# First pass, first four tiles: K and V computed chunk by chunk of Wk and Wv, eight tiles of x in buffers of their own

## The reference

```
src = layernorm(x)
q, k, v = src @ Wq + bq, src @ Wk + bk, src @ Wv + bv     # 16 heads of 64
Q, K = elu(q) + 1, elu(k) + 1
KV = einsum('bshd,bshm->bhdm', K, v)                       # sum over all rows
Z  = 1 / (einsum('bshd,bhd->bsh', Q, K.sum(axis=1)) + eps)
o  = einsum('bshd,bhdm,bsh->bshm', Q, KV, Z) @ Wo + bo
x1 = layernorm(src + o) * g1 + be1
u  = layernorm(x1 + gelu(x1 @ W1 + b1) @ W2 + b2) * g2 + be2
xa = x + u
out = xa + layernorm(xa) @ Wf.T + pooled(layernorm(xa)) @ disha
```

## Time and profile before

| | us |
|---|---|
| time, median of 3 runs (lowest, highest) | 1622.37 (1622.12, 1623.51) |
| the profiled execution's own time | 1624.31 |
| its span on the slowest core (core 5), first to last instruction | 1622.8 |
| spans of the eight cores | 1617.1 to 1622.8 |
| PE busy in the span | 1539.5 (95%) |

### The profile page before, as it was taken

How to read it: one execution, slowest core, us unless ns; L and a number is a source line. 1 busy time by engine, 2 the same in 40 slices (tenths; PEclk the granted TensorE clock), 3 DMA queues, 4 the chain that set the end, 5 groups by cost and what they waited for, 6 DMA issues and landing times.

```text
span 1622.8 us, 28100 instructions; the slowest of 8 cores (1617.1 to 1622.8 us)
## 1 busy us (share of the span) xinstructions
PE 1539.5 (95%) x9892; PEld 928.7 (57%) x9892; DVE 928.4 (57%) x1042; ACT 598.4 (37%) x1010; POOL 502.7 (31%) x438
## 2 busy tenths in 40 slices
PE   2699999999789999999999999999999999999995
PEld 1254544554356666666666666666666666666662
DVE  1466665665626574756657474755657475665314
ACT  1244555544533233333323333342323333332321
POOL 3464544545344222222222222222122222222101
PEclk9799999999899999999999999999999999999998
DMA  9776655457772201111110201111120111111011
...
DMA packets 52183, 135.60 MB, mean 84 GB/s; under 512 B 5968, under 2 KB 14160, under 8 KB 52048
## 3 DMA queue, kind: packets, MB, share of 16 engines
...
## 4 chain that ended last, share of the span: by engine, by line
PE 92%; issue 2%; DVE 2%; DMA 2%; POOL 1%; ACT 1%; SPq 0%; DVEq 0%; ACTq 0%; POOLq 0%
PE psH L1100 27%; PE psY L1081 27%; PE psY L444 13%; PE psS L673 7%; PE psS L493 6%; PE psS L415 6%; PE psS L659 1%; PE psS L547 1%; PE psH L423 1%; DMA qt_s<-arena 1%; PE psS L436 1%; PE psS L568 1%; DMA arena<-x 1%; PE psY L415 1%; PE psY L493 0%
## 5 line engine op out<-in xcount | busy, mean ns | idle before, releaser
L1100 PE MATMUL psH<-arena 128*128 128x256 bf16 x4096 | 531.6, 273 | 1.4 <-ACT arena L558 1.4
L1081 PE MATMUL psY<-arena 128*128 128x512 bf16 x2048 | 525.8, 379 | 0.4 <-DVE arena L601 0.4
L1006 ACT ACTIVATE arena<-psH,arena 128x256 bf16<-128x256 f32 x512 | 243.4, 475 | 733.3 <-PE psH L1100 731.4
L1100 PEld LDWEIGHTS psH<-arena 128*128 128x128 bf16 x4096 | 398.5, 98 | 131.0 <-issue 1.6
L1081 PEld LDWEIGHTS psY<-arena 128*128 128x128 bf16 x2048 | 200.3, 98 | 133.7 <-issue 1.6
L444 PE MATMUL psY<-arena 128*128 128x512 bf16 x1024 | 236.5, 386 | 16.3 <-DMA arena<-Wk 10.1
L589 DVE RECIPROCAL arena<-arena 128x512 f32<-128x512 f32 x56 | 187.4, 3346 | 29.8 <-ACT arena L579 29.8
L444 PEld LDWEIGHTS psY<-arena 128*128 128x128 bf16 x1024 | 100.2, 99 | 135.1 <-issue 25.6
L680 DVE TENSOR_TENSOR arena<-psS,arena 128x512 f32<-128x512 f32 x64 | 44.1, 689 | 168.1 <-PE psS L673 168.1
L502 DVE TENSOR_TENSOR arena<-psS,arena 128x512 f32<-128x512 f32 x60 | 41.3, 689 | 151.6 <-PE psS L493 151.4
L673 PE MATMUL psS<-arena 128*128 128x512 bf16 x512 | 122.2, 383 | 2.6 <-ACT arena L668 2.6
...
## 6 DMA issues: line engine op xcount, KB each, us to landing
arena<-x SPq DMA_DIRECT2D x64, 512.0 KB, 4.3
xb_s<-arena SPq DMA_DIRECT2D x32, 512.0 KB, 3.4
...
arena<-xb_s SPq DMA_DIRECT2D x32, 512.0 KB, 3.2
out<-arena SPq DMA_DIRECT2D x32, 512.0 KB, 2.9
arena<-qt_s SPq DMA_DIRECT2D x16, 512.0 KB, 3.2
...
```

What stands on the lines that cost most here:

```text
L1006: sc.activation(hT[n % 3][:, :], hbank[n % 2], AF.Gelu, bias=b1c[:, c:c + 1]).then_inc(b_g, 1)
L1081: ii = te.matmul(ybank[k], hT[n % 3][:, (k // 2) * P:(k // 2 + 1) * P], w2_v[c][:, (k % 2) * HALF:(k % 2 + 1) * HALF], start=(c == 0), sto ...
L1100: ii = te.matmul(hbank[n % 2], w1_v[c // NCH][:, w, (c % NCH) * P:(c % NCH + 1) * P], x1T[i % 2][:, w, :], start=(w == 0), stop=(w == NCH ...
```

## The change: what it does

Loads and buffers: tiles 2 to 7 of x get buffers of their own (`xe`, in the part of SBUF in which W2's chunks 16 to 27 land later), so that SP issues x0 to x3 at the start, x4 and x5 once Wk is in, x6 and x7 once Wv is in. The rows be2 and three small constants are issued after Wv has landed and no longer at the start. For tiles 0 to 7 be2 is added in place in the x buffer, after that tile's norm, and stored from there; `xbst` is used from tile 8 on. On POOL the four first k_sum come ahead of all x_be2. Tiles 1 and 3 get their own z and e buffers (`zf1`, `ebf1`), tiles 2 and 3 their own K buffers (`kx`).

Weights: each chunk of Wk and Wv has its own semaphore. PE takes chunk w for tiles 0 and 1 as it lands (`part`: two matmuls), with K of tile 2 following from chunk 5 on, then K of tile 3; V of tiles 0 and 1 by chunk of Wv; then V of tiles 2 and 3, and tile 4. For these tiles K and V lie in psK, psV and psH in turn. From tile 5 on the loop over tiles is the old one.

```diff
 def k_bank(t): return [psK, psV, psH.ap(), psK][t] if t < 4 else psK      # new
 def v_bank(t): return [psV, psH.ap(), psK, psV][t] if t < 4 else psV      # new
...
 def sync_a(sy):
-    for t in range(T):
-        if t >= 2:
-            sy.wait_ge(a_xb, t - 1)
-            sy.dma_start(xb_d[t - 2], xbst[:, :]).then_inc(s_xbst, 16)
-            sy.wait_ge(a_src, t - 1)
-        sy.dma_start(xbuf[t % 2][:, :], x_d[t * P:(t + 1) * P, :]).then_inc(s_x[t % 2], 16)
...
+    for t in range(1, 4):
+        x_load(t)
+    for dst, src in [(bqc, bqc_d), (bk1b, bkb_d)]:
+        sy.dma_start(dst[:, :], src).then_inc(s_const, 16)
+    sy.wait_ge(s_wk[NCH - 1], 16)
+    x_load(4)
+    x_load(5)
+    sy.wait_ge(s_wv[NCH - 1], 16)
+    for dst, src in [(be2b, be2_d), (onesb, one_d), (b1c, b1_d), (bvc, bvc_d)]:
+        sy.dma_start(dst[:, :], src).then_inc(s_rows, 16)
+    x_load(6)
+    x_load(7)
+    for t in range(8):
+        x_keep(t)
         if t == 1:
+            for u in range(2):
+                sy.wait_ge(s_x01[u], 16)
+                sy.wait_ge(a_src, u + 1)
+                x_load(8 + u)
+    for t in range(10, T):
+        x_keep(t - 2)
+        sy.wait_ge(a_src, t - 1)
+        x_load(t)
...
 def pool_a(gp):
     def x_be2(t):
...
+        if t >= 9:
+            gp.wait_ge(s_xbst, 16 * (t - 8))
+        if t < 8:
+            gp.wait_ge(a_src, t + 1)
+        gp.tensor_tensor(xbst[:, :] if t >= 8 else x_buf(t)[:, :], x_buf(t)[:, :],
+                         be2b[:, :], ALU.add).then_inc(a_xb, 1)
...
+    for t in range(4):
+        k_sum(t)
     x_be2(0)
     x_be2(1)
     for t in range(T):
         if t + 2 < T:
             x_be2(t + 2)
-        k_sum(t)
+        if t >= 4:
+            k_sum(t)
...
 def pe_a(te):
+    def part(t, w, ps, wgt, done):
+        for nh in range(2):
+            ii = te.matmul(ps[:, nh * 512:(nh + 1) * 512],
+                           srcT[0][:, w, t * P:(t + 1) * P],
+                           wgt[:, w, nh * 512:(nh + 1) * 512],
+                           start=(w == 0), stop=(w == NCH - 1))
+        if w == NCH - 1:
+            ii.then_inc(done, 1)
+
     src_tr(0)
-    for t in range(T):
+    src_tr(1)
+    for w in range(NCH):
+        if w == 0:
+            te.wait_ge(a_ev, 2)
+        te.wait_ge(s_wk[w], 16)
+        part(0, w, k_bank(0), wk_v, a_k)
+        part(1, w, k_bank(1), wk_v, a_k)
+        if w == 4:
+            src_tr(2)
+        if w == 5:
+            te.wait_ge(a_ev, 3)
+            for u in range(6):
+                part(2, u, k_bank(2), wk_v, a_k)
+        if w >= 6:
+            part(2, w, k_bank(2), wk_v, a_k)
+    src_tr(3)
+    te.wait_ge(a_ev, 4)
+    te.wait_ge(a_z, 1)
+    proj(3, k_bank(3), wk_v, a_k)
+    te.wait_ge(a_z, 3)
+    for w in range(NCH):
+        te.wait_ge(s_wv[w], 16)
+        part(0, w, v_bank(0), wv_v, a_v)
+        part(1, w, v_bank(1), wv_v, a_v)
+    src_tr(4)
+    te.wait_ge(a_z, 4)
+    proj(2, v_bank(2), wv_v, a_v)
+    te.wait_ge(a_vb, 2)
+    kv_sum(te, 0)
+    proj(3, v_bank(3), wv_v, a_v)
+    kv_sum(te, 1)
+    src_tr(5)
+    te.wait_ge(a_ev, 5)
+    te.wait_ge(a_vb, 3)
+    proj(4, psK, wk_v, a_k)
+    kv_sum(te, 2)
+    te.wait_ge(a_vb, 4)
+    proj(4, psV, wv_v, a_v)
+    kv_sum(te, 3)
+    te.wait_ge(s_wq, 16 * NCH)
+    q_proj(te, 0)
+    q_proj(te, 1)
+    for t in range(5, T):
```

More of the change, by code:

```diff
@@ L98, in build_nc @@
         ebf = VB(W + 51200, D)
+        xe = [VF(2048 * (16 + 2 * k), D) for k in range(6)]
+        kx = [VB(2048 * 28, D), VB(2048 * 29, D)]
+        zf1, ebf1 = VF(2048 * 14, D), VB(2048 * 30, D)
         slot = [VF(W + 4096 * k, D) for k in range(6)]
@@ L204, in qbuf, with k_bank, v_bank @@
             return qs1 if j == 1 else qs
+        def k_bank(t):
+            return [psK, psV, psH.ap(), psK][t] if t < 4 else psK
+        def v_bank(t):
+            return [psV, psH.ap(), psK, psV][t] if t < 4 else psV
         q_last = [sbank[0], ybank[2], sbank[0], ybank[3]]
@@ L210, in q_bank, with x_buf @@
             return sbank[0] if n < NCH * (NG - 2) else q_last[n % 4]
[L215 to L227 removed]
+        def x_buf(t):
+            return xe[t - 2] if 2 <= t < 8 else xbuf[t % 2]
@@ new lines, in k_buf, with z_buf, e_buf, x_done @@
+        def k_buf(t):
+            return kx[t - 2] if t in (2, 3) else kbf[t % 2]
+        def z_buf(t):
+            return zf1 if t in (1, 3) else zf
+        def e_buf(t):
+            return ebf1 if t in (1, 3) else ebf
+        def x_done(eng, t):
+            if 2 <= t < 8:
+                eng.wait_ge(s_xe[t - 2], 16)
+            else:
+                eng.wait_ge(s_x[t % 2], 16 if t < 2 else 16 * (t // 2 - 2))
+        def k_free(eng, t, done):
+            if t >= 6:
+                eng.wait_ge(done, t - 1)
+            elif t >= 4:
+                eng.wait_ge(done, t - 3)
@@ L316, in act_a @@
             evac(0)
-            for t in range(T):
-                if t + 1 < T:
+            evac(1)
+            rstd(2)
+            rstd(3)
+            evac(2)
+            evac(3)
+            for t in range(4):
+                k_exp(t)
+            rstd(4)
+            rstd(5)
+            v_out(0)
+            v_out(1)
+            evac(4)
+            v_out(2)
+            v_out(3)
+            evac(5)
+            sc.wait_ge(a_mem, 6)
+            for t in range(4, T):
+                if 5 <= t < T - 1:
                     evac(t + 1)
-                if t + 2 < T:
+                if 5 <= t < T - 2:
                     rstd(t + 2)
@@ L325, in act_a @@
                     q_store(sc, t // 4 - 2, 1)
+                k_exp(t)
+                if 5 <= t < T - 4:
+                    q_exp(sc, 2 * (t - 4))
                 if t == 4:
-                    sc.wait_ge(a_mem, 6)
-                k_exp(t)
-                if 4 <= t < T - 4:
-                    q_exp(sc, 2 * (t - 4))
+                    rstd(6)
                 v_out(t)
-                if 4 <= t < T - 4:
+                if t == 4:
+                    q_exp(sc, 0)
+                if t < T - 4:
                     q_exp(sc, 2 * (t - 4) + 1)
@@ L386, in dve_a @@
             norm(1)
+            stats(2)
+            stats(3)
+            norm(2)
             v.wait_ge(s_const, 32)
@@ L389, in dve_a @@
             v.tensor_scalar(bq1c[:, :], bqc[:, :], 1.0, None, ALU.add).then_inc(a_mem, 1)
-            stats(2)
-            for t in range(T):
-                if t + 2 < T:
+            norm(3)
+            k_in(0)
+            k_in(1)
+            k_out(0)
+            k_in(2)
+            k_out(1)
+            k_in(3)
+            k_out(2)
+            k_out(3)
+            stats(4)
+            stats(5)
+            norm(4)
+            norm(5)
+            for t in range(4, T):
+                if 5 <= t < T - 2:
                     norm(t + 2)
@@ L395, in dve_a @@
                 k_out(t)
-                if 4 <= t < T - 4:
+                if t == 4:
+                    stats(6)
+                    norm(6)
+                if t < T - 4:
                     q_out(v, 2 * (t - 4))
```

94 lines of the change are left out of this document (47 added, 47 removed).

## The result

The changed kernel takes 1608.98 us (median of 4 runs, 1608.0 to 1609.15), the kernel before 1622.24 us in 4 runs taken beside it (1622.12 to 1623.51). The ratio is 0.9915, 95% interval 0.9898 to 0.9932: faster by 13.3 us (0.8%), clear of the noise. The forecast was 1594.9 us with a range of 1588 to 1604, so the sign was right and the gain was half of the 27.4 us expected.

A forecast was written before the change was run, and what follows sets the result against it. PE's work bounds from tile 5 on; before, PE idles 46.4 us. Core 6's K of tile 5 moves from 94.75 to 66.5 us, ending at 1593.9; plus 1.4 spread, plus 1.5, minus 1.9 gives 1594.9 us, range 1588 to 1604.

The forecast's parts named there:

- K5: Start of K of tile 5 on PE, forecast at 66.5 us in place of 97.6 on core 5.
- the bound by which the small constants pay for x2: Loads at the start: moving the small constants away makes up for loading x2, so Wk lands at 26.2 us.
- rival 1: Wq gets half the DMA engines, lands at 68.5 us; K of tile 5 at 74.9, time 1603.3 us; chance 12%.
- rival 2: V of tiles 0 and 1 also at half clock, ending at 52.2 us, 7.2 late; time 1601 us; chance 6%.
- waits of PE on Wk and Wv in several short pieces: Expected sign in the profile after: PE waits briefly for weight chunks, ending near 28 and 44 us.
- Supply of x: Loop, x10 on: load, add, store, norm chain over 11.25 us a tile stalls PE; 1633 us at 13; chance 3%.
- 1 us of room at norm(6): DVE after K of tile 4: norm(6) done 1 us before src_tr(6) needs it at 66 us, costing nothing.
- The in-place add costs POOL what the old one did: POOL, tiles 0 to 7: adding be2 within the x buffer was taken to cost no extra time.
- a stall of 0 to 2 us: PE at src_tr(4), waiting for norm(4) on DVE, expected about 45 us; stall of 0 to 2 us.
- 1.4 us for the slowest core: Spread of the new tile 5 start between cores: half of the old 2.8 us, added to 1593.9 for 1595.3.
- The forecast's own case: Whole kernel: the forecast holds with a time of 1588 to 1599 us; chance 73%.
- rivals 1 to 3: Rival 1, rival 2, and a larger gain: K of tile 5 at 63.7, 1590.7 us; below 1588, chance 4%.

The follow-up runs named there:

- tiny adds: The changed kernel with POOL's in-place adds of be2 for tiles 0 to 7 covering one column of 1024, waits and stores kept; 1601.68 us, ratio 0.9866.
- be2 early: The changed kernel with be2 loaded behind x5 on its own semaphore, POOL's first adds waiting for it alone; 1602.09 us, ratio 0.9855.
- ACT order: The changed kernel with v_out(4) and q_exp(0) put ahead of rstd(6) in ACT's list; 1605.1 to 1605.9 us, ratio 0.9891.

## Why the prediction was right in sign and wrong in size

**Right.** The account of what bounds the kernel held: PE's work from tile 5 on is unchanged (297.1 to 297.5 us from K5 to the middle part on every core before, and on the four late cores after), and the gain is how much earlier the loop is done. Wk had landed by 25.87 us, when SP issues x4 (forecast 27.9, lower bound 26.2), and Wv by 41.78, when it issues be2 (forecast 43.7):

```profile
25.87 0.81 SPq L258 DMA_DIRECT2D arena<-x  x2
41.78 0.33 SPq L280 DMA_DIRECT2D arena<-be2r  x1
```

Both are 2 us early, as the bound by which the small constants pay for x2 would have it. Wq is seen where PE gets to it in time: its waits end at 59.1 to 62.0 us in the later experiments (forecast 62.6), so rival 1, Wq at 68.5, did not come. Rival 2, half clock until tile 3's V, did not come either: the granted clock over the first 81 us is 0.92, and K of tile 3 takes 3.61 us for 16 matmuls, the time at full clock. But its premise was not put to the test, nor did the "waits of PE on Wk and Wv in several short pieces" come: PE waited for Wk on no core and for Wv 0.7 us at most (core 2), since it started on chunks that had landed and was slow at first. Supply of x never held up PE in the loop. The W2 and Wo loads gave nothing back.

**Wrong, the step that decides.** "norm(6) comes behind K of tile 4 on DVE: ... k_in, k_exp, k_out, stats, rstd and norm take 7 to 9 us ... All of this costs nothing on that count, with 1 us of room at norm(6)", and with it "The in-place add costs POOL what the old one did". The add does cost POOL the same (2.36 us each), but not DVE. k_out was priced by its usual 1.2 us, and took 8.35 on core 4 beside adds in a row. In place of 1 us of room there was a 9.48 us wait, and it fell on q_proj(1), which the forecast took to run back to back with q_proj(0): it waits for a PSUM bank through q_exp(0), and ACT's list has rstd(6) ahead of that. So the step has two parts: k_out(4) held up for 7.1 us, and 2.4 us of waiting for the bank that come even without that, as tiny adds shows. Tiny adds (the wait down to 2.36 us) and be2 early (6.8 us back, nothing left out) show that it was the adds; ACT order shows how the wait reaches PE. The forecast had a hint in its own figures: it gives norm as 0.8 to 3.0 us and did not ask what made the long ones.

**Wrong, the smaller terms, on core 4.** The forecast had PE at the first q_proj at 61.5 us, and it was there at 65.55. Of these 4.0 us, 2.8 are src_tr(4), at 47.78 in place of 45.0 ("a stall of 0 to 2 us" was 3.41), and 1.3 the half clock that followed (48.59: 16 matmuls in 4.53 us). Wq's wait of 1.1 us fell away behind it. After the long wait q_proj and src_tr ran at half clock (granted 0.50 from 76 to 80 us): 3.37 and 0.85 us from start to start in place of 1.73 and 0.45, 2.0 us. So 66.5 + 4.0 - 1.1 + 9.5 + 2.0 = 80.9, with 81.14 measured. The forecast allowed 1.4 us for the slowest core; 81.14 - 67.9 = 13.2 us more than that gives 1594.9 + 13.2 = 1608.1, with 1608.98 measured. The remaining 0.9 us are two small terms: the median is 0.2 us below the profiled execution and not 1.9, and core 4 needs 1526.5 us from K5 to its end where core 6 had needed 1527.4 (1.7 us up, 0.9 down).

**Also missed.** On cores 0, 1, 2 and 7, K5 came at 72.1 to 73.5, and the forecast's rule that a gain at K5 stays until the end failed there: q_out(0) at 6.39 us let PE stand in the loop, "any wait of PE in the loop" being named as a sign of a wrong prediction. Two more of its signs came: src_tr(4) waited 3.41 us, and weight loads 0.43 us apart stood past 45 us. The forecast looked for a loss on such a wait only in the supply of x.

**Slips in the working that decide nothing.** The 15.0 us of be2r over four transfers are 3.75 us each and not 4.1, which moves the upper bound of Wk from 30.3 to 29.95 us. The slow stretch after an idle one is given as 4 to 5 us each; by the 5.04 us of the 16 matmuls at 38.57 it was near 3 there (our estimate, from 0.43 and 0.216 us a matmul). The forecast's own case and rivals 1 to 3 add up to 95% and not 94.

**Open.** What decides whether a waiting DVE instruction gets in between two adds is not settled. On core 0 k_out(4) started at 64.08 during an add and ended at once behind it, on core 4 at 64.21, during a DMA issue of POOL, and was passed by two adds. On core 3 it started at 65.32 during an add and ended only at 71.62. No run isolates that, nor whether the DMA issues between the adds hold it up as well. Nor is it shown why some instructions are held up and others never are (last section).
